# Two edits to a fused fp32 kernel on one core: a diagonal product in the selective scan, and turns ahead of a convolution

## The reference

```python
# layer 0: deformable 3x3 convolution of 180 channels, two of them (f_w, f_h) with offsets of their own
val = gather(y0, x0, (1-dy)*(1-dx)) + gather(y0, x0+1, (1-dy)*dx) + gather(y0+1, x0, dy*(1-dx)) + gather(y0+1, x0+1, dy*dx)
out = einsum('bikhw,oik->bohw', val.reshape(Bx, C, 9, H, W), weight)
...
# layer 3: selective scan, 384 channels (d), 16 states (n), 9216 positions (t), 2 images
def step(h, inp):
    u_t, d_t, B_t, C_t = inp
    dA = exp(d_t[..., None] * A)
    h = dA * h + (d_t * u_t)[..., None] * B_t[:, None, :]
    return h, einsum('bdn,bn->bd', h, C_t)
y = ys + D * x_conv
out = einsum('bdl,cd->bcl', y * silu(z), W_out)
```

## Time and profile before

| | |
|---|---|
| median of three runs | 11887.78 us |
| the profiled execution | 11906.47 us, span 11904.5 us |
| PE busy | 10560.3 us (89%) |
| ACT busy | 10408.0 us (87%) |
| DVE busy | 9752.1 us (82%) |
| POOL busy | 5061.3 us (43%) |
| mean granted TensorE clock | 0.952 |

### The profile page before, as it was taken

One profiled execution on the slowest core, in us unless ns is written; L12 is line 12 of the kernel. 1 busy time (PEld: TensorE's weight loads), 2 busy tenths in 40 slices (PEclk: granted clock), 3 DMA queues, 4 the chain that ended last, 5 costly groups with the idle time before them and its releaser, 6 DMA issues. The chain is left out here.

```text
span 11904.5 us, 346184 instructions
## 1 busy us (share of the span) xinstructions
PE 10560.3 (89%) x137398; PEld 8743.9 (73%) x137398; DVE 9752.1 (82%) x14111; ACT 10408.0 (87%) x10534; POOL 5061.3 (43%) x3633
## 2 busy tenths in 40 slices
PE   6689999999999999999999999881599888888888
PEld 4479999999999999999999895430443377777776
DVE  4578888888888888888888787789878799999998
ACT  3289999999999999999999995397768799999999
POOL 0033333343333333333333331033300188888888
PEclk9899999999999999999999996895799899999999
DMA  6488888888888888888888888444644433333333
GB/s 166 131 220 213 217 220 214 216 217 217 213 213 218 216 213 217 217 212 214 212 215 215 211 214 215 138 156 139 171 132 159 145 107 114 109 112 112 105 118 91
DMA packets 818455, 2128.59 MB, mean 179 GB/s; under 512 B 145698, under 2 KB 414368, under 8 KB 674496
## 3 DMA queue, kind: packets, MB, share of 16 engines
q1 hardware_dynamic: 800912, 2072.13, 64.7%
q10 hardware_dynamic: 15120, 30.71, 0.7%
q0 software_dynamic: 832, 3.59, 0.1%
HBM read 1782.85 MB, written 323.30 MB: 177 GB/s over the span
## 5 line engine op out<-in xcount | busy, mean ns | idle before, releaser
L884 PE MATMUL dc_p<-dc_t 96*64 96x90 f32 (+1 forms) x103896 | 4665.1, 247 | 160.0 <-PEq L879 79.4
L884 PEld LDWEIGHTS dc_p<-dc_t 96*64 96x64 f32 x103896 | 4376.7, 137 | 435.8 <-issue 433.7
L955 POOL TENSOR_TENSOR dc_t<-dc_t 128x324 f32<-128x324 f32 (+1 forms) x2885 | 2593.1, 899 | 4050.6 <-DVEq L1043 2727.6
L1019 DVE TENSOR_TENSOR dc_t<-dc_p,dc_t 128x810 f32<-128x810 f32 (+1 forms) x2886 | 3044.6, 1055 | 903.4 <-DVEq L1016 868.4
L831 ACT ACTIVATE dc_t<-dc_t 96x2304 f32<-96x2304 f32 x1447 | 3189.2, 2204 | 122.0 <-ACTq L830 119.9
L836 ACT ACTIVATE dc_t<-dc_t 96x2304 f32<-96x2304 f32 x1446 | 3049.6, 2109 | 0.0
L2582 DVE TENSOR_TENSOR_SCAN ms_t<-ms_t,ms_p 128x512 f32<-128x512 f32 x1728 | 2076.9, 1260 | 191.5 <-ACT ms_t L2447 109.9
L2470 POOL TENSOR_TENSOR ms_t<-ms_t 128x1536 f32<-128x1536 f32 x576 | 1987.5, 3462 | 319.6 <-DVE ms_t L2582 310.8
L925 PE MATMUL dc_p<-dc_t 128*128 128x180 f32 (+1 forms) x7488 | 1539.3, 338 | 0.9 <-issue 0.6
L2496 PE MATMUL ms_p<-top_t,ms_t 128*128 128x128 f32 x6912 | 1078.9, 279 | 406.1 <-ACT ms_t L2440 316.7
L925 PEld LDWEIGHTS dc_p<-dc_t 128*128 128x128 f32 (+1 forms) x7488 | 1140.4, 190 | 174.0 <-issue 5.7
(11 more groups left out here) (263 smaller groups left out, 9816.9 us busy)
## 6 DMA issues: line engine op xcount, KB each, us to landing
dc_t<-sxd SPq DMA_DIRECT2D x1447, 864.0 KB, 6.1
ms_t<-bcd SPq DMA_DIRECT2D x576, 256.0 KB, 3.3
dc_t<-xrT SPq DMA_DIRECT2D x49, 675.0 KB, 9.8
kvd<-wk_t SPq DMA_DIRECT2D x18, 1536.0 KB, 5.1
szd<-mi_t SPq DMA_DIRECT2D x36, 768.0 KB, 4.4
xvd<-mi_t SPq DMA_DIRECT2D x36, 768.0 KB, 4.7
dld<-mi_t SPq DMA_DIRECT2D x36, 768.0 KB, 3.4
ms_t<-dld SPq DMA_DIRECT2D x36, 768.0 KB, 4.5
```

The source lines that it names most:

```text
L884: ins = e.matmul(PT[j % 2][o:o + 64, t // 3, t % 3 * nr * CG:(t % 3 + 1) * nr * CG], HX[:, m // 2 % RP, m % 2, t * 128 + o:t * 128 + o + 6 ...
L955: e.tensor_tensor(ZH[:, n % 4, :, 0:m], z[:, :, 0:m], z[:, :, nr * CG - m:nr * CG], ALU.add)\
L1019: e.tensor_tensor(Zt[:, n % 4, 0:nr * LEN].rearrange("p (b m i) -> p b m i", b=3, i=CG), PT[n % 2][:, :, 0:3 * nr * CG].rearrange("p b (m ...
```

## The change

```diff
+                def turn(n):
+                    conv, g = n // NG % 2, n % NG // 2
+                    e.wait_ge(s_va, 2).then_inc(s_va, -2)
...
+                turn(0)
+
                 def body(b, y2, w):
                     for n in range(0, NBB, 2):
...
                         for m in (n + LEAD, n + LEAD + 1):
                             e.wait_ge(s_pt, 1).then_inc(s_pt, -1)
                             sample(m % NBB)
                         e.wait_ge(s_vt, 1).then_inc(s_vt, -1)
+                        turn((n + 2) % NBB)
...
-                    if n == 8 and 0 <= c and c + 2 < NC:
+                    if n == 4 and c >= 1:
+                        store(c - 1)
+                        if c + 1 < NC:
+                            load_x(c + 1)
+                    if n == 11 and 0 <= c and c + 2 < NC:
                         e.wait_ge(s_yz, ND * (c + 1))
                         load(c + 2)
...
-                    for tb in range(TB):
-                        ins = e.activation(BU[:, i % RT, tb, :], UT[:, c % 2, tb, 0:DI], ACT.Copy,
+                    for tb in range(TS):
+                        e.activation(BU[:, i % RT, tb, :], UT[:, c % 2, tb, 0:DI], ACT.Copy,
+                                     scale=UT[:, c % 2, tb, DI + n:DI + n + 1])
+                    for tb in range(TS, TB):
+                        ins = e.activation(DG[:, i % RT, tb - TS, :], k.ident[:, :], ACT.Copy,
                                            scale=UT[:, c % 2, tb, DI + n:DI + n + 1])
...
-                    if n == 10 and c + 1 < NC:
+                    if n == 8 and c + 1 < NC:
                         gain(c + 1)
...
-                    if tb >= 2:
-                        e.wait_ge(s_ev, TB * c + tb - 1)
+                    if c + tb > 0:
+                        e.wait_ge(s_ev, TB * c + tb)
...
+                    for tb in range(TS, TB):
+                        ins = e.matmul(PB[:, d, tb * 128:(tb + 1) * 128],
+                                       UT[:, i // NS % 2, tb, d * 128:(d + 1) * 128], DG[:, i % RT, tb - TS, :],
+                                       start=True, stop=True)
...
+                        if d == 0 and 10 <= n < 10 + TB and c + 1 < NC:
+                            turn_gain(c + 1, n - 10)
+                        if d == 1 and n == 2 and c >= 1:
+                            turn_back(c - 1, 0)
+                        if d == 2 and n in (3, 4) and c >= 1:
+                            turn_back(c - 1, n - 2)
+                        if d == 2 and 6 <= n < 9 and c >= 1:
+                            project(c - 1, n - 6)
+                        if d == 2 and 10 <= n < 13 and c >= 1:
+                            project(c - 1, n - 7)
+                        if d == 2 and 13 <= n < 13 + ND and c < NC:
+                            add_skip(c, n - 13)
...
-                    if n == 10 and c >= 1:
-                        put(c - 1)
+                        if d == 0 and n == 3 and c >= 1:
+                            gate(c - 1, 0)
+                        if d == 1 and n in (4, 5) and c >= 1:
+                            gate(c - 1, n - 3)
+                        if d == 2 and n in (9, 13) and c >= 1:
+                            put(c - 1, (n - 9) // 4)
```

More of the change, by code:

```diff
@@ L904, in _ @@
                 e.wait_ge(s_w, 16).then_inc(s_w, -16)
+                def turn(n):
+                    conv, g = n // NG % 2, n % NG // 2
+                    e.wait_ge(s_va, 2).then_inc(s_va, -2)
+                    for u, c in enumerate(pieces[g]):
+                        o = min(128, NG * LEN - 128 * c)
+                        ins = e.transpose(PR[0:o, u * 128:(u + 1) * 128],
+                                          VA[:, conv, 128 * c:128 * c + o], k.ident[:, :])
+                    if g == 2:
+                        ins = turn_sum((n - 14) // NB % NRB, conv ^ 1)
+                    ins.then_inc(s_tr, 1)
+                turn(0)
                 def body(b, y2, w):
@@ L2410, in unload @@
                     e.wait_ge(s_pt, TB * c + tb + 1)
-                    e.activation(UT[:, c % 2, tb, :], PO[:, tb % 2, 0:WT], ACT.Copy).then_inc(s_ev, 1)
+                    e.activation(UT[:, c % 2, tb, :], PO[:, 1, 0:WT], ACT.Copy).then_inc(s_ev, 1)
                 def carry(i):
@@ L2428, in _ @@
                     c, n = i // NS, i % NS
-                    if n == 14 and c + 1 < NC:
-                        unload(c + 1, 0)
-                        unload(c + 1, 1)
+                    if n in (13, 14) and c + 1 < NC:
+                        unload(c + 1, n - 13)
                     if n == 15 and c + 1 < NC:
@@ L2494, in turn @@
                         e.wait_ge(s_scan, ND * (i - 1) + d + 1)
-                    for tb in range(TB):
-                        ins = e.transpose(PB[:, d, tb * 128:(tb + 1) * 128], BU[:, i % RT, tb, d * 128:(d + 1) * 128],
-                                          k.ident[:, :])
+                    for tb in range(TS):
+                        e.transpose(PB[:, d, tb * 128:(tb + 1) * 128], BU[:, i % RT, tb, d * 128:(d + 1) * 128],
+                                    k.ident[:, :])
+                    for tb in range(TS, TB):
+                        ins = e.matmul(PB[:, d, tb * 128:(tb + 1) * 128],
+                                       UT[:, i // NS % 2, tb, d * 128:(d + 1) * 128], DG[:, i % RT, tb - TS, :],
+                                       start=True, stop=True)
                     ins.then_inc(s_db, 1)
@@ L2520, in turn_back @@
                     e.wait_ge(s_cp, ND * c + d + 1)
-                    if d == 0:
-                        e.wait_ge(s_ev, min(TB * (c + 2), TB * NC))
-                    if d == 2:
-                        e.wait_ge(s_yz, ND * c + 1)
+                    if d == 0 and c >= 1:
+                        e.wait_ge(s_xo, 2 * c)
+                    if d >= 1:
+                        e.wait_ge(s_yz, ND * c + d)
                     for tb in range(TB):
-                        ins = e.transpose(PO[:, d % 2, tb * 128:(tb + 1) * 128], YS[:, d, tb * 128:(tb + 1) * 128],
+                        ins = e.transpose(PO[:, 0, tb * 128:(tb + 1) * 128], YS[:, d, tb * 128:(tb + 1) * 128],
                                           k.ident[:, :])
@@ L2533, in project @@
                         e.wait_ge(s_yz, ND * (c + 1))
[L2534 removed]
+                    if j == ND:
+                        e.wait_ge(s_xo, 2 * c + 1)
+                    ins = e.matmul(PO[0:HC, 0, :], WO[:, d, m * HC:(m + 1) * HC], YY[:, d, :],
                                    start=(d == 0), stop=(d == ND - 1))
[L2536 removed]
+                    if d == ND - 1:
                         ins.then_inc(s_po, 1)
```

74 lines of the change are left out of this document (23 added, 51 removed).

## The result

The changed kernel takes 12046.14 us (median of 4 runs, 12012.72 to 12057.92), beside 11892.01 for the kernel before: a ratio of 1.0123 [1.011, 1.0135]. It is slower, and outside the range of 11795 to 11925. Its profiled execution has a span of 12040.3 us, against 11904.5.

What follows compares the result with a forecast made beforehand. PE was taken to bound sampling and ACT the scan. Sampling -48 and scan +23 sum to -25 us: 11881.5 against the profiled 11906.5, or 11863 on the median 11887.8; range 11795 to 11925.

Steps and rivals of the forecast that it cites:

- The product: Scan: a real diagonal product replaces a transpose on PE, 0.218 us instead of 0.109; ACT's fourth copy shrinks to 0.28.
- if the load came in time: Scan: product 8 would end at T6+17.5, before DVE needs it; period 65.45 us, -1.6 a chunk, -56 us.
- some 2: Scan's end with one bank: some 2 us longer, as a projection's half waits for an addition.
- the moved loads: Scan: loads behind spread 11 land at T6+13.35, POOL idles 2.75 us; period 67.75 us, +24 over 34 chunks.
- From +20.4 PE is the bound: Scan iterations 10 to 12: PE needs 4.4 us each against DVE's 3.53; rest of iteration 10 takes 3.9.
- Sampling: Turn ahead of the convolution saves 0.05 us a pair, 72 us; later row loads cost 24: -48 us.
- rival C: Scan: product at its upper bound or landing 0.5 us later; chunk 69, scan +70, total 11910 us; chance 0.14.
- DVE's row wait at 1.9 to 2.0 us: Sampling: expected sign that DVE's wait for row loads, 1.76 us each before, becomes 1.9 to 2.0.
- A: Scan: late loads hurt little; scan -30 to -85, total 11755 to 11810 us; chance 0.22.
- B: Sampling: row loads set the pace; sampling +0 to +24, scan +23, total 11911 to 11935 us; chance 0.17.
- D: Scan: ACT pays a fixed part for small copies, so the product does not replace the copy's time; 11875 us; chance 0.05.
- The page's fit: Scan loads: 2 us plus bytes over 436 GB/s gives 7.5 us instead of 9.1; chunk 66.15, -31 us.

Runs made afterwards that it cites:

- loads at 8: Changed kernel with SP issuing the next chunk's loads at n = 8 again instead of 11: 11787.69 us, ratio 0.9917 to the kernel before.
- The kernel with PE kept busy: Changed kernel plus 36 unused identity transposes on PE ahead of the sum that waits for product 8: 11963.54 us, ratio 1.0059 to the kernel before.
- the two halves: Changed kernel with only its sampling edit, or only its scan edits: 11855.13 us (ratio 0.9969) and 12056.38 us (1.0141) to the kernel before.
- the earlier release: Changed kernel, loads at n = 8, last unload later, SP's next pair load released at the turn's first transpose: 11735.34 us, beside 11736.33 without.

## Why the prediction was wrong

**Where it held.** The places and their order were right, their sizes from the landing on were not. Counted from T6 = 10545.36, SP issues the loads at +4.05, as forecast. POOL waits for a DMA before each gain, DVE's scan 11 and PE for product 8 (DVE 3.9 us, where 2.1 stood), ACT for PE at the fourth unload and now at all four. The product takes 0.23 us from its start to the sum's (10560.88 to 10561.11), a turn 0.55 (10560.56 to 10561.11) and ACT's diagonal 0.29 (10561.14 to 10561.43); the forecast had 0.218, 0.545 and 0.28. The product is thus two transposes long, as the rows had it, and not four. From T15 to T6 it is 10545.36 - 10516.70 = 28.66 us; the forecast had 28.7. And "if the load came in time" it had 65.45: with loads at 8 it is 65.1. The tail grew by 3.7 us, for which "some 2" stood, and the first and the last chunk shrank by 2.5 and 3.8, not 1.5.

**The step that failed** is the moved loads: "the spread ahead in the same queue adds about 0.2: +13.35. POOL has finished product 7 at +10.6 and stands idle 2.75 us." The 0.2 was an estimate with no row behind it, and the two kernels with loads ahead of and behind a spread show it at 2.1 us. The kernel before does not show it for these loads: nothing was issued in the 11 us ahead of them. POOL idles 4.7 us (median), and product 8 ends at T6+21.6 in the chunk shown, T6+22.2 in the one before it, not at +20.3.

**The term that was missing** is the clock. "From +20.4 PE is the bound", with 3.9 us for the rest of iteration 10, was reckoned at the full clock that the earlier trace rows shows for the whole scan. But the chain itself gives PE a wait of 4.7 us just there, and behind it PE runs at the lower level: 6.2 us instead of 3.9. The kernel with PE kept busy gives 1.9 us a chunk back. The clock alone would have turned the sign: with the loads ahead of the spread the landing is the 9.1 us of the forecast and POOL idles no more than forecast, and the chunk is 69.7 instead of 67.75, the kernel slower than before (ratio 1.0047). A clock of 1.00 in the trace of before held only as long as no such wait stood in the loop, and the prediction added one.

**The sum.** 65.1 with loads in time; 4.7 for POOL's idle time (69.8 in the kernel with PE kept busy, 65.7 at an idle time of 0.63: one for one); 1.9 for the clock: 71.7. The forecast had 65.45, 2.3 for the wait and nothing for the clock, 67.75. On the mean the chunk is 71.9, 4.2 more than that; in 34 chunks this is 142 us of the 183 by which 11863 was missed. Sampling adds 15 and the kernel before, at 11892 instead of 11888, 4; the first and last chunk and the tail take off 2. Some 24 us are left over, about what the measurements scatter by (the intervals of the two halves are 13 and 19 us to each side, that of the whole 15).

**The forecast's shape.** The chain's places were worked out to a tenth, but its one unmeasured size, the landing behind a spread, got no bounds of its own; rival C allowed "a landing 0.5 later". Each us of landing costs 34 us, and the range took in no more than that half.

**Sampling**: -48 was forecast, -33 measured. The gain a pair was right. I grouped the pairs of each trace by their shapes; those that nothing holds up take 4.031 us instead of 4.076, 4.229 for 4.276, 4.336 for 4.381, and 4.445 for 4.490 in the kind that also turns the sums (on the smaller tile): 0.045 each, 65 us over 1440. What lies above these lengths is waiting, and it grew: 187 to 221 us in the three traces without the edit, 227 to 255 in the ten with it, 36 more on the mean. The largest part, some 15 us, falls on the kind with the turn of the sums: of its 192 pairs 73 to 75 were held up without the edit, and 92 to 103 with it where the release was left as it was. The forecast put the loss down to the row loads: "DVE's row wait at 1.9 to 2.0 us" came true (281.0 us in 142 waits). With the earlier release that wait shrank and this kind of pair lost 64 us instead of 84, but the other pairs waited 40 us more, and the time was the same. So the size was near by luck, since its cause is not shown: what holds the other pairs stays open, and no run took down ACT's work, which fills 6192.99 of the 6500 us.

**The rivals.** A (loads hurt little) fell: POOL does wait. B fell: sampling gained. C named a product at its upper bound and a later landing; the product was at its middle, and the landing later by four times what C had. D fell: ACT's copy costs 0.29, and its iteration is 3.75. None of the four named the clock.

**The page's fit.** The Trainium skill, "DMA: Bandwidth & Descriptors", Anatomy of one DMA, would give 7.5 us for these loads by its fit, an estimate; the page states the fit for one DMA on the gpsimd path, and these are four from SP. The runs here show 9.1 with an idle queue and 11.3 behind a spread. The measurement decides. By the page the loads would have hurt less than forecast; they hurt more.

## What to carry to other kernels

Before a load is moved later, find how long it takes to land behind what will then stand just ahead of it in its queue, not how long it takes today, and bound that number from above if no row shows it. A stall that a change puts into a tightly fed TensorE can be paid twice, once as the wait and once as slow matmuls behind it; a clock of 1.00 in the trace of before says nothing of the kernel with the stall. A cheaper operation on the busiest engine gives only what the next wait leaves: here ACT's saving of 3.5 us a chunk gave nothing in the old order, 1.95 us with the new order and the loads in time, and all of the 3.5 with one more instruction moved.

## What the runs showed of the hardware

- Four loads (2.39 MB) land 9.0 to 9.2 us from the first issue when nothing was issued in the 3.8 us or more ahead of them (medians of nine kernels), and 11.25 to 11.33 when a 256 KB spread to 128 partitions was issued just ahead in the same queue.
- After 4.7 us of waiting PE's granted clock was at 1.2 GHz, and its 128-column operations took twice as long for about 5 us of work. With 36 idle transposes in the wait it stayed at 2.4 GHz in 27 of 34 chunks.
- With waits of 2.4 to 4.4 us on PE, once a chunk (the loads ahead of the spread), the clock fell in all 34 chunks too, and cost 1.6 and 2.9 us in the two shown: about as much as the 1.9 behind the longer wait, where some 2 of the 6.8 us at the lower level pass while PE still waits.
- An fp32 matmul of 128 columns takes 0.22 us, a transpose 0.11: two to one. A copy of 128 columns on ACT takes 0.29 us, one of 3 columns 0.10.
